# A fused decoder layer on one core: the order of the last eight slots, written out by hand on four engines

## The chip, the cores and the metric

The kernel runs on 1 core of one Trainium2 chip. The metric is the device time of one execution in microseconds; the time of a version is the median of its runs. A smaller time is better.

## The reference

x is 4 x 512 tokens of 512 channels, float32. The layer has three stages, each followed by a residual and a layernorm without weights:

```python
# 1: attention: four products with quantised rows and ternary weights, a linear recurrence over the tokens
x = _layernorm(x + _L0_attn_ref(x, Wi, Wf, Wg, Wo, g_norm_weight))
# 2: each token has one of 4 experts, by its token id
g = silu(h @ ctx[e].T); u = h @ ctx[e].T; y = (g * u) @ ctx[e]      # 512 x 512 for each expert
x = _layernorm(x + y)
# 3: mixed = sum over the 8 factors of x @ factor, / sqrt(8) + bias
x = _layernorm(x + mixed)
```

In stage 2 the gate, the up and the down weights are the same matrix of the expert, so that one product gives g and u: hidden = silu(z) * z.

## The kernel before

**Tiles, groups, slots.** The 2048 tokens are 16 tiles of 128, in 8 groups of two. The attention stage runs group by group, with channels on the partitions for the recurrence. Its normalised rows are scattered to DRAM (`sorted_rows`) in an order in which each block of 128 rows belongs to one expert. Such a block is a slot. There are N_SLOTS = 19, since four experts can leave three blocks partly filled. Stages 2 and 3 run slot by slot.

**One slot n**, step by step, with the engine of each:

- `load_rows(n)` (SP, L207 to L212): a DMA of 128 rows into `rows[n % 4]`. It waits for `square_2(n - 4)` and `token_of_row(n - 4)`, which were the last to read that buffer, and for the scatters that fill the slot.
- `transpose_a(n)` (PE, L1427): four 128 x 128 transposes of the rows into a PSUM bank. From slot 11 on (TAIL = 11) the bank is `bank_a`, and the step waits for `low_a(n - 1)`; before that it is `bank_tr`, which it shares with `transpose_h`.
- `high_a(n)` (ACT, L614) and `low_a(n)` (DVE, L985): the bank is split into a rounded part a_hi and the rest a_lo, both fp32r.
- `up(n)` (PE, L1467): z = a times the slot's expert, twelve matmuls of 512 columns into `bank_z`: eight that need a_hi, then four that need a_lo. It waits for `hidden(n - 1)`.
- `silu_z(n)` (ACT, L623) and `hidden(n)` (DVE, L994): act_z = silu(z) * z.
- `transpose_h(n)` (PE), `high_h(n)` (ACT), `low_h(n)` (DVE), `down(n)` (PE, into `bank_y`): the same pattern for the second product.
- `residual_2(n)` (DVE, L998): y plus the rows, with a sum along the row, and a small operation that makes the mean. `square_2(n)` (ACT, L628): the sum of squares. `power_2(n)` (POOL, L322, three small operations at L312 to L314): the scale. `norm_2(n)` (ACT, L634): the layernorm, in place in `x2[n % 4]`.
- `transpose_m(n)` (PE, into `bank_q`), `high_m(n)` (ACT), `low_m(n)` (DVE), `mix(n)` (PE, into `bank_m`, waits for `residual_3(n - 1)`): the third product, with the sum of the factors.
- `add_bias(n)` (POOL, L350): adds the bias to x2, after `transpose_m(n)`. `token_of_row(n)` (POOL, L346): keeps the token numbers of the slot's rows.
- `residual_3(n)` (DVE, L1008), with its small mean, which waits for `mix(n)`, `add_bias(n)` and for the landing of `store(n - 2)`; `square_3(n)` (ACT, L641), `power_3(n)` (POOL), `norm_3(n)` (ACT, L647).
- `store(n)` (POOL, L355): an indirect DMA of the rows to the output.

**What sets the order.** Every engine has its own list of steps, written out in the code, and takes them strictly in that order; semaphores hold a step until what it reads is there. For the slots up to 10 the lists run beside the attention groups: a loop over `turn`, and then a hand-written piece for the last group. From slot 11 on each engine ran a loop over n, printed below in the function: on PE `up(n)`, `transpose_a(n + 1)`, `transpose_m(n - 2)`, `down(n - 1)`, `transpose_h(n)`, `mix(n - 2)`. In the last rounds of the loop only the steps remain whose slot exists: `up(18)`, `transpose_m(16)`, `down(17)`, `transpose_h(18)`, `mix(16)`; then `transpose_m(17)`, `down(18)`, `mix(17)`; then `transpose_m(18)`, `mix(18)`. On POOL a round of the loop was `power_3(n - 3)`, `add_bias(n - 2)`, `store(n - 3)`, `token_of_row(n + 1)`, `power_2(n - 1)`.

Of the kernel before, what the change touches and what calls it, by code (L numbers as in the profile page):

```python
# [74 lines left out]
def decoder_layer(nc, x, small_in, ctx_t, wf_t, wi_t, wg_t, wo_t, g_weight, factors, bias, out):  # L75
# [6 lines left out]
    with ExitStack() as whole:  # L82
# [105 lines left out]
        def is_slot_n(n):  # L188
            return 0 <= n < N_SLOTS

        with nc.Block() as block:
# [49 lines left out]
            def _(pool):  # L241
# [252 lines left out]
                add_bias(n - 1)  # L494
                token_of_row(n + 1)

                token_of_row(TAIL)
                for n in range(TAIL, N_SLOTS + 3):
                    if is_slot_n(n - 3):
                        power_3(n - 3)  # L500
                    if is_slot_n(n - 2):
                        add_bias(n - 2)
                    if is_slot_n(n - 3):
                        store(n - 3)
                    if is_slot_n(n + 1):
                        token_of_row(n + 1)
                    if is_slot_n(n - 1):
                        power_2(n - 1)
                pool.wait_ge(s.out0, 16 * ((N_SLOTS + 1) // 2))
                pool.wait_ge(s.out1, 16 * (N_SLOTS // 2))  # L510

# [1 line left out]
            def _(act):  # L513
# [335 lines left out]
                norm_2(n)  # L849
                norm_3(n - 2)  # L850

                silu_z(TAIL - 1)
                high_h(TAIL - 1)
                high_a(TAIL)
                for n in range(TAIL, N_SLOTS + 3):
                    if TAIL - 1 <= n - 2 and is_slot_n(n - 2):
                        norm_2(n - 2)
                    if is_slot_n(n - 3):
                        square_3(n - 3)
                    if is_slot_n(n):  # L860
# [12 lines left out]
            @block.vector  # L873
            def _(dve):
# [777 lines left out]
```

## Time and profile before

| what | value |
|---|---|
| median of 3 runs | 341.45 us (340.44 to 343.64) |
| profiled execution, its own time | 342.06 us |
| its span, first to last instruction | 340.3 us |
| mean granted TensorE clock over the span | 0.963 |
| PE busy | 278.1 us (82%), 1505 matmuls |
| DVE busy | 226.3 us (66%) |
| ACT busy | 229.6 us (67%) |
| POOL busy | 190.8 us (56%) |

Times in the trace count from the first instruction. "Busy" is the union of an engine's instructions. A start in the timeline is when an instruction began on its engine; consecutive matmuls overlap, so that their pace is read from the distance of the starts. What stands in brackets is how long the engine had been idle before the instruction and what released it. A clock of 1.00 is 2.4 GHz, one of 0.50 is 1.2 GHz.

### The profile page before, as it was taken

The page shows a single profiled execution, that of the slowest core. Times are in us where ns is not written, and L with a number is a line of the kernel's source. Part 1 is how long each engine was busy: PE and PEld are TensorE (multiplying, and loading weights), DVE is VectorE, ACT ScalarE, POOL GpSimd, SP SyncE. Part 2 cuts the span into 40 slices and gives each one's busy share as a digit, 9 for nine tenths or more (in the row PEclk, how much of TensorE's full clock was granted, in tenths as well). Part 3 has the DMA queues.
Part 4 walks back from the last instruction along what each step waited for, and adds up shares of the span by engine and source line. Part 5 has one row for each costly group of instructions (what it writes and reads, how often), then busy time and mean ns, then how long its engine had stood idle before and what let it go on. Part 6 is the DMA issues. An engine that isn't in the chain of part 4 may idle for free.

```text
span 340.3 us, 5734 instructions
## 1 busy us (share of the span) xinstructions
PE 278.1 (82%) x1505; PEld 211.9 (62%) x1518; DVE 226.3 (66%) x488; ACT 229.6 (67%) x456; POOL 190.8 (56%) x381
## 2 busy tenths in 40 slices
PE   1376646484879899999999998998999999999760
PEld 1253414252557678787778876676888888887540
DVE  2789999999987879968677696454543434543310
ACT  4687789889678769986887686476555644554530
POOL 2536765858637748865565856547444444454442
PEclk9999989879799999999999999999999999999975
DMA  7999981987593782013003002205111111000000
GB/s 233 387 388 387 225 196 62 185 153 143 130 227 79 115 179 65 1 62 126 0 33 141 17 15 111 62 7 186 56 40 56 62 66 62 33 26 29 4 6 0
DMA packets 17406, 37.02 MB, mean 109 GB/s; under 512 B 1503, under 2 KB 1631, under 8 KB 17376
## 3 DMA queue, kind: packets, MB, share of 16 engines
q0 software_dynamic: 6496, 15.74, 19.6%
q1 hardware_dynamic: 10880, 20.92, 19.2%
q8 instruction: 14, 0.23, 0.3%
q14 instruction: 16, 0.13, 0.1%
HBM read 26.68 MB, written 10.76 MB: 110 GB/s over the span
## 4 chain that ended last, share of the span: by engine, by line
PE 62%; ACT 9%; issue 5%; DVE 5%; DMA 2%; POOL 2%; ACTq 0%; POOLq 0%; DVEq 0%; SPq 0%
PE bank_y L1455 5%; PE bank_z L1455 5%; PE bank_y L1456 5%; PE bank_z L1456 5%; PE bank_z L1459 5%; PE bank_y L1459 5%; PE bank_m L1455 4%; PE bank_m L1456 4%; PE bank_m L1459 4%; PE bank_tr L1424 3%; PE bank_c L1357 2%; PE bank_q L1424 2%; PE bank_a L1357 1%; PE bank_b L1357 1%; DMA sorted_rows<-r,place 1%
## 5 line engine op out<-in xcount | busy, mean ns | idle before, releaser
L312 POOL TENSOR_SCALAR n_v<-n_dev 128x1 f32<-128x1 f32 (+1 forms) x46 | 8.8, 192 | 52.2 <-ACT x L644 26.7
L1455 PE MATMUL bank_y<-c_hi,h_hi 128*128 x76 | 31.8, 418 | 1.8 <-ACT h_hi L612 1.4
L996 DVE TENSOR_TENSOR act_z<-bank_z,act_z 128x512 f32<-128x512 f32 x19 | 13.1, 689 | 30.1 <-ACT act_z L626 30.1
L1455 PE MATMUL bank_m<-f_hi,m_hi 128*128 128x512 f32 x76 | 32.1, 423 | 0.8 <-ACT m_hi L612 0.8
L353 POOL TENSOR_TENSOR x<-x,bias_b 128x512 f32<-128x512 f32 x19 | 24.6, 1293 | 14.5 <-PE bank_q L1424 14.5
L1455 PE MATMUL bank_z<-c_hi,a_hi 128*128 x76 | 30.4, 400 | 2.8 <-ACT a_hi L612 1.5
L1456 PE MATMUL bank_m<-f_lo,m_hi 128*128 128x512 f32 x76 | 30.8, 405 | 0.0
L1456 PE MATMUL bank_y<-c_lo,h_hi 128*128 x76 | 30.1, 396 | 0.0
L1456 PE MATMUL bank_z<-c_lo,a_hi 128*128 x76 | 30.1, 395 | 0.0
L612 ACT ACTIVATE h_hi<-bank_tr 128x512 fp32r<-128x512 f32 x19 | 11.3, 596 | 26.7 <-PE bank_tr L1424 26.7
L313 POOL TENSOR_TENSOR n_d<-n_v,minus_half 128x1 f32<-128x1 f32 (+1 forms) x46 | 27.1, 588 | 3.8
L358 POOL DMA_INDIRECT out<-r,token_of x19 | 20.3, 1067 | 12.3 <-ACT r L651 7.6
L1013 DVE SCALAR_TENSOR_TENSOR r<-bank_m,x 128x512 f32<-128x512 f32 x19 | 13.1, 691 | 21.0 <-PE bank_m L1459 20.0
L1002 DVE SCALAR_TENSOR_TENSOR x<-bank_y,rows 128x512 f32<-128x512 f32 x19 | 13.1, 691 | 19.1 <-PE bank_y L1459 19.1
L638 ACT ACTIVATE x<-x,n_b,n_d 128x512 f32<-128x512 f32 x19 | 15.4, 810 | 12.2 <-POOL n_b L314 12.2
L1357 PE MATMUL bank_c<-xq_t,w_q 128*128 128x256 bf16 x128 | 18.3, 291 | 5.2 <-ACT mc_row L540 2.7
L343 POOL DMA_INDIRECT sorted_rows<-r,place x16 | 17.8, 1113 | 8.3 <-ACT r L594 5.7
L1459 PE MATMUL bank_m<-f_hi,m_lo 128*128 128x512 f32 x76 | 21.3, 403 | 0.0
L1459 PE MATMUL bank_y<-c_hi,h_lo 128*128 x76 | 20.6, 393 | 0.0
L1459 PE MATMUL bank_z<-c_hi,a_lo 128*128 x76 | 20.6, 393 | 0.0
L644 ACT ACTIVATE x<-r,n_mean 128x512 f32<-128x512 f32 x19 | 13.7, 720 | 9.6 <-DVE n_mean L1017 9.6
L626 ACT ACTIVATE act_z<-bank_z 128x512 f32<-128x512 f32 x19 | 11.2, 592 | 12.1 <-PE bank_z L1459 12.1
(205 smaller groups left out, 848.7 us busy)
## 6 DMA issues: line engine op xcount, KB each, us to landing
f_sum<-in_factors POOLq DMA_DIRECT2D x7, 1024.0 KB
rows<-sorted_rows SPq DMA_DIRECT2D x19, 256.5 KB, 2.9
xs<-in_x SPq DMA_DIRECT2D x8, 512.0 KB, 7.6
c_stage<-in_ctx_t SPq DMA_DIRECT2D x4, 1024.0 KB, 14.3
sorted_rows<-pad_row SPq DMA_DIRECT2D x1, 1539.0 KB, 18.3
w_stage<-in_wf_t SPq DMA_DIRECT2D x1, 1024.0 KB, 8.7
w_stage<-in_wi_t SPq DMA_DIRECT2D x1, 1024.0 KB, 10.8
w_stage<-in_wg_t SPq DMA_DIRECT2D x1, 1024.0 KB, 13.0
```

What stands on the lines that cost most here:

```text
L313: link(pool.tensor_tensor(d, v, minus_half[:, 0:v.shape[1]], ALU.pow), chain)
L343: pool.indirect_dma_start(sorted_rows, bass.IndirectOffsetOnAxis(place[:, u:u + 1], 0), r1[:, j, :], None).then_inc(s_scat[j], 16)
L353: pool.tensor_tensor(tile, tile, bias_b[:], ALU.add).then_inc(s.x2b, 1)
L358: pool.indirect_dma_start(out_rows, bass.IndirectOffsetOnAxis(token_of[:, n:n + 1], 0), r3[:, n % 2, :], None, bounds_check=B * S - 1, oob ...
L638: a.activation(r, r, ACT.Identity, bias=n2_b[:, n % 2:n % 2 + 1], scale=n2_d[:, n % 2:n % 2 + 1]).then_inc(s.x2, 1)
L644: a.activation(x2[:, n % RING, :], r3[:, n % 2, :], ACT.Square, bias=n3_mean[:, n % 2:n % 2 + 1], accum_out=n3_dev[:, n % 2:n % 2 + 1]).th ...
L996: v.tensor_tensor(act_z[:], bank_z[:], act_z[:], ALU.mult).then_inc(s.hid, 1)
L1357: last = t.matmul(bank[:, i * GW:(i + 1) * GW], w_q[:, m, d, ch:ch + P], xq_t[:, :, d, :], start=(d == 0), stop=(d == KC - 1))
L1424: last = t.transpose(bank[:, c * P:(c + 1) * P], src[:, c * P:(c + 1) * P], ident[:])
L1455: t.matmul(bank[:], hi[:, c, :], w_hi(c), start=(c == 0), stop=False)
L1456: t.matmul(bank[:], hi[:, c, :], w_lo(c), start=False, stop=False)
L1459: last = t.matmul(bank[:], lo[:, c, :], w_hi(c), start=False, stop=(c == KC - 1))
```

## The change

Each engine's loop over the last slots is replaced by a written list of the same steps. No step is added or dropped and no wait, buffer or tile is changed: each engine issues the same instructions with the same semaphore counts, in another order. On PE `transpose_a(11)` now comes ahead of `transpose_h(10)`, `transpose_m(9)` ahead of `up(11)`, the transposes of the next rows stand right behind `up`, and at the end `transpose_m(17)` and `mix(17)` stand behind `down(18)`. The diff, with the indentation taken off and several of the new lines put into one:

```diff
@@ -1601,22 +1735,61 @@
-mix(TAIL - 3)
-transpose_h(TAIL - 1)
-transpose_a(TAIL)
-for n in range(TAIL, N_SLOTS + 2):
-    if is_slot_n(n):
-        up(n)
-    if is_slot_n(n + 1):
-        transpose_a(n + 1)
-    if is_slot_n(n - 2):
-        transpose_m(n - 2)
-    if is_slot_n(n - 1):
-        down(n - 1)
-    if is_slot_n(n):
-        transpose_h(n)
-    if is_slot_n(n - 2):
-        mix(n - 2)
+ mix(8); transpose_a(11); transpose_h(10); transpose_m(9); up(11); transpose_a(12); down(10); mix(9)
+ transpose_a(13); transpose_h(11); up(12); down(11); transpose_m(10); transpose_h(12); up(13)
+ transpose_a(14); mix(10); transpose_m(11); down(12); transpose_h(13); up(14); transpose_a(15); mix(11)
+ down(13); transpose_h(14); transpose_m(12); up(15); transpose_a(16); mix(12); transpose_h(15); down(14)
+ transpose_m(13); up(16); transpose_a(17); mix(13); transpose_h(16); transpose_m(14); down(15); up(17)
+ transpose_a(18); mix(14); transpose_m(15); down(16); up(18); transpose_h(17); mix(15); transpose_m(16)
+ down(17); transpose_h(18); mix(16); down(18); transpose_m(17); mix(17); transpose_m(18); mix(18)
@@ -849,26 +887,82 @@
-silu_z(TAIL - 1)
-high_h(TAIL - 1)
-high_a(TAIL)
-for n in range(TAIL, N_SLOTS + 3):
-    if TAIL - 1 <= n - 2 and is_slot_n(n - 2):
-        norm_2(n - 2)
-    if is_slot_n(n - 3):
-        square_3(n - 3)
-    if is_slot_n(n):
-        silu_z(n)
-    if is_slot_n(n + 1):
-        high_a(n + 1)
-    if is_slot_n(n - 2):
-        high_m(n - 2)
-    if is_slot_n(n - 3):
-        norm_3(n - 3)
-    if is_slot_n(n):
-        high_h(n)
-    if is_slot_n(n - 1):
-        square_2(n - 1)
+ silu_z(10); high_a(11); high_h(10); square_3(8); high_a(12); high_m(9); silu_z(11); square_2(10)
+ norm_3(8); norm_2(10); high_h(11); silu_z(12); square_3(9); high_a(13); high_m(10); high_h(12)
+ square_2(11); norm_2(11); high_a(14); high_m(11); silu_z(13); square_3(10); norm_3(9); high_h(13)
+ silu_z(14); norm_3(10); square_2(12); high_a(15); norm_2(12); high_m(12); square_2(13); high_h(14)
+ square_3(11); high_a(16); silu_z(15); norm_2(13); norm_3(11); square_3(12); high_h(15); square_2(14)
+ high_m(13); silu_z(16); norm_2(14); high_a(17); high_m(14); norm_3(12); square_3(13); high_h(16)
+ square_2(15); silu_z(17); norm_2(15); high_m(15); high_a(18); norm_3(13); square_2(16); square_3(14)
+ silu_z(18); norm_2(16); high_h(17); norm_3(14); high_m(16); square_2(17); high_h(18); square_3(15)
+ norm_2(17); square_3(16); norm_3(15); high_m(17); square_2(18); norm_3(16); norm_2(18); high_m(18)
+ square_3(17); norm_3(17); square_3(18); norm_3(18)
@@ -1283,22 +1377,62 @@
-hidden(TAIL - 1)
-low_h(TAIL - 1)
-low_a(TAIL)
-for n in range(TAIL, N_SLOTS + 3):
-    if is_slot_n(n - 3):
-        residual_3(n - 3)
-    if is_slot_n(n):
-        hidden(n)
-    if is_slot_n(n + 1):
-        low_a(n + 1)
-    if is_slot_n(n - 2):
-        low_m(n - 2)
-    if is_slot_n(n - 1):
-        residual_2(n - 1)
-    if is_slot_n(n):
-        low_h(n)
+ hidden(10); low_h(10); low_a(11); residual_3(8); hidden(11); low_a(12); low_m(9); residual_2(10)
+ residual_3(9); low_h(11); hidden(12); residual_2(11); low_a(13); low_m(10); low_h(12); low_a(14)
+ hidden(13); residual_3(10); low_h(13); residual_2(12); low_m(11); residual_3(11); hidden(14)
+ residual_2(13); low_a(15); low_h(14); low_m(12); hidden(15); low_a(16); residual_3(12); residual_2(14)
+ low_m(13); low_h(15); hidden(16); residual_3(13); residual_2(15); low_a(17); low_h(16); low_m(14)
+ low_a(18); hidden(17); low_m(15); residual_2(16); residual_3(14); hidden(18); residual_3(15); low_h(17)
+ low_m(16); residual_2(17); low_h(18); residual_3(16); residual_2(18); low_m(17); residual_3(17); low_m(18)
+ residual_3(18)
@@ -494,18 +494,56 @@
-token_of_row(TAIL)
-for n in range(TAIL, N_SLOTS + 3):
-    if is_slot_n(n - 3):
-        power_3(n - 3)
-    if is_slot_n(n - 2):
-        add_bias(n - 2)
-    if is_slot_n(n - 3):
-        store(n - 3)
-    if is_slot_n(n + 1):
-        token_of_row(n + 1)
-    if is_slot_n(n - 1):
-        power_2(n - 1)
+ power_3(8); add_bias(9); power_2(10); token_of_row(11); token_of_row(12); store(8); add_bias(10)
+ token_of_row(13); power_2(11); power_3(9); add_bias(11); token_of_row(14); token_of_row(15); store(9)
+ power_3(10); store(10); power_2(12); power_2(13); power_3(11); add_bias(12); add_bias(13); store(11)
+ power_2(14); add_bias(14); power_3(12); power_2(15); store(12); power_3(13); store(13); add_bias(15)
+ power_2(16); power_3(14); token_of_row(16); store(14); add_bias(16); power_2(17); token_of_row(17)
+ power_3(15); power_3(16); store(15); power_2(18); add_bias(17); store(16); add_bias(18); power_3(17)
+ token_of_row(18); store(17); power_3(18); store(18)
```

The four parts are those of PE, ACT, DVE and POOL. SP's list of loads is unchanged.

## Rows read from the trace of the kernel before

**Rows 1.** Busy time of the engines by stage: stretch, sum, PE, PEld, DVE, ACT, POOL, clock, DMA.
```profile
237.60:311.60 74.00, 74.00 (x365) 60.91 (x366) 32.72 (x76) 39.01 (x75) 34.02 (x68) 1.00 0.14 49
...
311.60:329.50 17.90, 15.12 (x61) 11.07 (x59) 5.51 (x16) 7.97 (x15) 9.01 (x17) 0.90 0.05 18
```

**Rows 2.** Timeline of TensorE, slot 11: start, us, what [idle before, releaser].
```profile
236.16 0.66 PE L1424 MATMUL bank_a<-small,rows 128*128 128x128 f32 x4 [0.40 <-DMA rows<-sorted_rows]
...
237.60 0.49 PE L1455 MATMUL bank_z<-c_hi,a_hi 128*128 x1 [0.78 <-ACT a_hi L612]
...
240.48 0.60 PE L1424 MATMUL bank_a<-small,rows 128*128 128x128 f32 x4
...
241.27 0.48 PE L1455 MATMUL bank_y<-c_hi,h_hi 128*128 x1
...
244.50 0.48 PE L1455 MATMUL bank_m<-f_hi,m_hi 128*128 128x512 f32 x1
...
247.38 0.39 PE L1455 MATMUL bank_z<-c_hi,a_hi 128*128 x1
...
250.17 0.60 PE L1424 MATMUL bank_a<-small,rows 128*128 128x128 f32 x4
```

**Rows 3.** Timeline of TensorE at the end.
```profile
313.87 1.10 PE L1459 MATMUL bank_m<-f_hi,m_lo 128*128 128x512 f32 x4
...
315.67 0.66 PE L1424 MATMUL bank_q<-small,x 128*128 128x128 f32 x4 [0.70 <-ACT x L638]
...
316.43 0.49 PE L1455 MATMUL bank_y<-c_hi,h_hi 128*128 x1
...
319.31 0.39 PE L1455 MATMUL bank_m<-f_hi,m_hi 128*128 128x512 f32 x1
...
323.43 0.66 PE L1424 MATMUL bank_q<-small,x 128*128 128x128 f32 x4 [1.14 <-ACT x L638]
...
324.86 0.47 PE L1455 MATMUL bank_m<-f_hi,m_hi 128*128 128x512 f32 x1 [0.78 <-ACT m_hi L612]
```

**Rows 4.** Timeline of DVE, ACT and POOL at the end.
```profile
319.51 0.69 DVE L1002 SCALAR_TENSOR_TENSOR x<-bank_y,rows 128x512 f32<-128x512 f32 x1 [1.56 <-PE bank_y L1459]
...
320.44 0.72 ACT L631 ACTIVATE rows<-x,n_mean 128x512 f32<-128x512 f32 x1 [1.58 <-DVE n_mean L1006]
...
322.56 0.81 ACT L638 ACTIVATE x<-x,n_b,n_d 128x512 f32<-128x512 f32 x1 [1.31 <-POOL n_b L314]
...
324.12 0.60 ACT L612 ACTIVATE m_hi<-bank_q 128x512 fp32r<-128x512 f32 x1
...
329.48 0.69 DVE L1013 SCALAR_TENSOR_TENSOR r<-bank_m,x 128x512 f32<-128x512 f32 x1 [4.04 <-PE bank_m L1459]
...
331.38 0.19 POOL L312 TENSOR_SCALAR n_v<-n_dev 128x1 f32<-128x1 f32 x1 [3.33 <-ACT x L644]
```

**Rows 5.** Busy time by stretch; PE's granted clock stands third from the end.
```profile
325.50:325.75 0.25, 0.25 (x3) 0.15 (x2) 0.00 (x0) 0.25 (x1) 0.25 (x1) 0.50 0.00 0
```

**Rows 6.** Timeline of ACT and DVE, slot 17.
```profile
298.84 0.60 ACT L626 ACTIVATE act_z<-bank_z 128x512 f32<-128x512 f32 x1 [1.06 <-PE bank_z L1459]
...
299.47 0.69 DVE L996 TENSOR_TENSOR act_z<-bank_z,act_z 128x512 f32<-128x512 f32 x1 [2.54 <-ACT act_z L626]
...
300.08 0.68 DVE L983 TENSOR_TENSOR a_lo<-bank_a,a_hi 128x512 fp32r<-128x512 f32 x1
```

**Rows 7.** Timeline: the small mean on DVE, beside POOL's add_bias and alone.
```profile
221.99 1.28 POOL L353 TENSOR_TENSOR x<-x,bias_b 128x512 f32<-128x512 f32 x1 [1.61 <-PE bank_q L1424]
222.02 1.27 DVE L972 TENSOR_SCALAR n_mean<-n_sum 128x2 f32<-128x2 f32 x1
...
320.25 0.15 DVE L1006 TENSOR_SCALAR n_mean<-n_sum 128x1 f32<-128x1 f32 x1
```

**Rows 8.** Line 358 (store): its issue on POOL, and from issue to landing.
```profile
326.99 1.07 POOL L358 DMA_INDIRECT out<-r,token_of  x1 [0.41 <-issue]
...
DMA to landing us min/median/max: 2.2/2.8/5.3
```

More of the change, by code:

```diff
@@ L495, in _ @@
                 token_of_row(n + 1)
-                token_of_row(TAIL)
-                for n in range(TAIL, N_SLOTS + 3):
-                    if is_slot_n(n - 3):
-                        power_3(n - 3)
-                    if is_slot_n(n - 2):
-                        add_bias(n - 2)
-                    if is_slot_n(n - 3):
-                        store(n - 3)
-                    if is_slot_n(n + 1):
-                        token_of_row(n + 1)
-                    if is_slot_n(n - 1):
-                        power_2(n - 1)
+                power_3(8)
+                add_bias(9)
+                power_2(10)
+                token_of_row(11)
+                token_of_row(12)
+                store(8)
+                add_bias(10)
+                token_of_row(13)
+                power_2(11)
+                power_3(9)
+                add_bias(11)
+                token_of_row(14)
+                token_of_row(15)
+                store(9)
+                power_3(10)
+                store(10)
+                power_2(12)
+                power_2(13)
+                power_3(11)
+                add_bias(12)
+                add_bias(13)
+                store(11)
+                power_2(14)
+                add_bias(14)
+                power_3(12)
+                power_2(15)
+                store(12)
+                power_3(13)
+                store(13)
+                add_bias(15)
+                power_2(16)
+                power_3(14)
+                token_of_row(16)
+                store(14)
+                add_bias(16)
+                power_2(17)
+                token_of_row(17)
+                power_3(15)
+                power_3(16)
+                store(15)
+                power_2(18)
+                add_bias(17)
+                store(16)
+                add_bias(18)
+                power_3(17)
+                token_of_row(18)
+                store(17)
+                power_3(18)
+                store(18)
                 pool.wait_ge(s.out0, 16 * ((N_SLOTS + 1) // 2))
@@ L850, in _ @@
                 norm_3(n - 2)
[L852 to L871 removed]
+                silu_z(10)
@@ new lines, in _ @@
+                high_a(11)
+                high_h(10)
+                square_3(8)
+                high_a(12)
+                high_m(9)
+                silu_z(11)
+                square_2(10)
+                norm_3(8)
+                norm_2(10)
+                high_h(11)
+                silu_z(12)
+                square_3(9)
+                high_a(13)
+                high_m(10)
+                high_h(12)
+                square_2(11)
+                norm_2(11)
+                high_a(14)
@@ new lines, in _ @@
+                high_m(11)
+                silu_z(13)
+                square_3(10)
+                norm_3(9)
+                high_h(13)
+                silu_z(14)
+                norm_3(10)
+                square_2(12)
+                high_a(15)
+                norm_2(12)
+                high_m(12)
+                square_2(13)
+                high_h(14)
+                square_3(11)
+                high_a(16)
+                silu_z(15)
+                norm_2(13)
+                norm_3(11)
@@ new lines, in _ @@
+                square_3(12)
+                high_h(15)
+                square_2(14)
+                high_m(13)
+                silu_z(16)
+                norm_2(14)
+                high_a(17)
+                high_m(14)
+                norm_3(12)
+                square_3(13)
+                high_h(16)
+                square_2(15)
+                silu_z(17)
+                norm_2(15)
+                high_m(15)
+                high_a(18)
+                norm_3(13)
+                square_2(16)
@@ new lines, in _ @@
+                square_3(14)
+                silu_z(18)
+                norm_2(16)
+                high_h(17)
+                norm_3(14)
+                high_m(16)
+                square_2(17)
+                high_h(18)
+                square_3(15)
+                norm_2(17)
+                square_3(16)
+                norm_3(15)
+                high_m(17)
+                square_2(18)
+                norm_3(16)
+                norm_2(18)
+                high_m(18)
+                square_3(17)
@@ L873, in _ @@
+                norm_3(17)
+                square_3(18)
+                norm_3(18)
             @block.vector
```

110 lines of the change are left out of this document (added).

## The prediction

> **What bounds the kernel now.** The numbers are read in four steps. First the busy time by stage: from 237.60 to 311.60, while the slots from 11 on run, PE is busy 74.00 of 74.00 us at the full granted clock, and DVE, ACT and POOL are busy less than 40 us each [rows 1]. So what bounds the last eight slots is TensorE's own work, and no order of the same instructions can shorten it; it can only take away idle PE at the two ends. From 311.60 to 329.50 PE is idle 2.8 of 17.9 us [rows 1].
>
> Second, one slot of PE [rows 2]. A product (12 matmuls of 512 columns) takes 2.88 behind a transpose (237.60 to 240.48, and 244.50 to 247.38) and 2.79 behind another product (247.38 to 250.17). Two groups of four transposes ahead of a product take 0.79 (240.48 to 241.27); with the 0.09 by which the product behind them is longer that is 0.44 a group, 0.35 of it before the product starts. Three products and three groups make 9.69 a slot (240.48 to 250.17); I use 2.79 and 0.44 throughout. The reader is to see also that the first transpose of slot 11 starts at 236.16 because its rows landed only then, and that up(11) follows 1.44 later, after ACT has made a_hi (0.78 of that is put down to ACT).
>
> Third, the drain on PE [rows 3]. mix(16) would hand over at 313.87 + 0.92 = 314.79, but the transpose of m(17) starts at 315.67: 0.88 idle, 0.70 of it put down to ACT's norm. down(18) starts 0.76 after that, where 0.35 is usual: 0.40 more. mix(17) runs from 319.31, then PE waits until 323.43 for m(18) and until 324.86 for m_hi.
>
> Fourth, who makes it wait [rows 4]. From down(18)'s end at 319.31: residual at 319.51 (+0.20), square at 320.44 (+0.93), norm at 322.56 (+2.12, POOL's three small steps in it), transpose at 323.43 (+0.87), m_hi at 324.12 (+0.69), mix(18) at 324.86 (+0.74): 5.55 together. Then mix(18) itself is slow. From its start at 324.86 to residual_3 at 329.48 it takes 4.62, where down(18) took 316.43 to 319.51, or 3.08, for the same twelve matmuls [rows 3, 4]. The reason stands in the windows: from 325.50 the granted clock is 0.50 [rows 5], so most of mix(18) ran at 1.2 instead of 2.4 GHz. Before the fall PE had been without work from 322.10 (319.31 + 2.79) to 323.43 and again from the end of the transposes to 324.86. The low clock costs 1.54.
>
> **The change part by part.** No instruction is added or taken away; the counts of products, transposes, DMAs and elementwise operations are the same, so all that counts is where each queue waits.
>
> Start. transpose_h(10) and transpose_m(9) now stand behind transpose_a(11), which sits until 236.16. They run at 236.60 and 237.04 in the 1.44 that PE waits for a_hi anyway [rows 2]. h(10) had been in the wait for the rows; m(9) had cost 0.44 inside the slot. Gain 0.44. x(9) is long ready, since norm_2(9) is issued before the tail. On DVE low_h(10) still stands ahead of low_a(11): h_hi is made only at about 237.9, so a_lo(11) is done at about 239.2, and up(11) asks for it after 8 matmuls of 0.233, at 239.46. Margin 0.2.
>
> Middle. I walked PE through the new list without gaps: up(11) 237.60, down(10) 240.84, mix(9) 243.71, up(12) 247.30, up(13) 253.76, up(14) 263.45, up(15) 273.14, up(16) 282.83, up(17) 292.60, up(18) 301.85, down(17) 308.23, mix(16) 311.46, down(18) 314.33, its end 317.12 (all that follows counts from this walk; the 0.25 found below shifts all together). For each transpose I then followed its operand through ACT, DVE and POOL in their new orders, with 0.60 from one DVE operation to the next, 0.63 from silu_z to hidden [rows 6], 0.49 for a copy on ACT (estimate: the 0.60 of a copy overlaps the next start by about 0.1, as on DVE), 0.72 for a square or norm, and 2.12 from square to norm [rows 4]. Most operands have over half a microsecond to spare. The tight ones: transpose_m(12), because store(10) now stands ahead of power_2(12) on POOL (norm_2(12) at 271.8, transpose possible at 272.7, nominal 272.78); a_lo(17), because low_a(17) waits behind residual_2(15) (done 294.4, asked 294.46); up(18), which asks for hidden(17), and that stands behind low_a(18), high_a(18) and high_m(15) (done 301.7, nominal 301.85); h_hi(18) behind square_2(17) (margin 0.6). None of these is over its time.
>
> One thing is. The small mean behind a residual takes 0.15 alone (320.25), but one of its kind takes 1.27 where it starts inside POOL's add_bias: 222.02 against 221.99 + 1.28 [rows 7]. Before, the tail has no such meeting. In the walk the new order has three: the mean of slot 11 (at 253.9, in add_bias(10), 253.6 to 254.9), of slot 14 (283.4, in add_bias(13), 283.2 to 284.4) and the third mean of slot 14 (303.9, in add_bias(15)). Each holds DVE for 0.4 to 1.05. At slots 14 nothing behind it is due. At slot 11 low_a(13) comes at 255.1 instead of 254.1 and is done at 255.8, where up(13) asks for it at 253.76 + 1.86 = 255.62: PE loses 0.25 with the hand-off. I cost the middle at 0.25. Lower bound 0 (the meeting is missed by some tenths); upper bound four slips of 0.5, or 2.0, since what PE loses there it never gets back.
> The Trainium skill (SBUF — State Buffer, Who interferes with whom) says that VectorE in its two-port modes, which a tensor_scalar can enter, and GpSimd take a shared pair of ports by turns, each for a whole instruction, and that an operation with one input in SBUF outside these modes does not meet GpSimd. The trace agrees: the mean waits until add_bias is over, the residual and hidden, whose other input is a PSUM bank, never do. By this rule the three meetings are real and the time is the sum below; without it, it would be 0.25 lower.
>
> SP's queue: rows(n) asks for square_2(n-4) and token_of_row(n-4). These stay at least 7 us ahead of transpose_a(n) in the walk; a cost of 0. Of the stores, residual_3(n) asks that store(n-2) has landed: 2.8 us in the median, at most 5.3 [rows 8]. store(15) starts at about 318.0 in the walk, lands at 320.8, and is asked at 321.6; at 5.3 it would cost 1.7.
>
> Up to down(18)'s end. Before, 319.31. Less the idle 0.88 and 0.40, less m(9)'s 0.44, less m(17)'s 0.44, which now comes behind down(18): 317.15 (the walk gives 317.12). Gain 2.19. This is a gain only if the middle holds.
>
> Behind down(18). Now: transpose_m(17) at once, 1.43 to mix(17) as from 323.43 to 324.86, mix(17) 2.87, transpose_m(18), 1.43 to mix(18): 5.73, against 5.55 before. x(18) takes 4.1 from down(18)'s end, and high_m(17) on ACT (copy from 317.8) stands just ahead of square_2(18) (wanted 318.25): no loss, 0.1 to spare. store(15) ahead of power_2(18) ends at 319.1 and the power is wanted at 319.3. So mix(17) no longer covers all of the last chain, and the last chain covers mix(17): loss 0.18, mix(18) at 322.85.
>
> The clock. In the new order PE's idle stretches here are 317.8 to 318.55, and after mix(17) about 322.1 to 322.85, with matmuls of 2.87 between. Before the fall at 325.50 there was 1.3 and 0.8 of idle with only four transposes between [rows 3, 5]. I take it that the clock stays full: mix(18) takes 3.08 to residual_3 instead of 4.62, gain 1.54. Bounds: 0 (falls as early in mix(18) as before) and 1.54.
>
> Last queue. POOL's list ends add_bias(17), store(16), add_bias(18), power_3(17), store(17), power_3(18), store(18). With 1.28 for add_bias [rows 7], 0.41 + 1.07 for a store [rows 8], 1.15 for a power (2.12 less the 0.97 from square to POOL: 1.90 from residual_3 to power_3 less 0.93 [rows 4]), power_3(17) ends at 325.7, norm_3(17) at 326.5, store(17) runs until 328.4. residual_3(18) is at 325.93, so power_3(18) is wanted at 327.83 and gets POOL at 328.4: loss 0.6. Before, store(17) was away at 326.99 + 1.07, long before 331.38 [rows 4, 8]. From power_3(18) to the end nothing changes.
>
> Sum: -2.19 + 0.25 + 0.18 - 1.54 + 0.6 = -2.70. The profiled execution took 342.06 with a span of 340.3, so the new one is 339.4 with a span of 337.6. The median of the runs is 341.45, 0.6 below the profiled one; part of that may be that the clock falls later or not at all in other runs. I keep 339.4 as the time, 2.05 or 0.6% under the median.
>
> **The rivals.**
> A. More than 1% faster: POOL is free for power_3(18) in time (my 0.6 is too much), no mean meets an add_bias, and the timed runs of before all lose the clock as the profiled one: 341.45 - 2.70 - 0.6 - 0.25 = 337.9. For it: POOL is busy only 34.02 of 74.00 [rows 1]. Against: five POOL operations stand in a row, each near its time.
> B. The clock falls in mix(18) all the same: 339.4 + 1.5 = 340.9. For it: two waits of 0.75 stay. Against: a whole mix between them.
> C. The middle leaks. Three queues now have margins of 0.1 to 0.6 at the places named above. With the upper bound of the middle, 2.0 in place of 0.25, the time is 341.1, and the change shows nothing. For it: the hand-offs are added up from single rows, each good to some 0.05. Against: a slip moves all queues together, so that several do not add up fully.
> D. Slower. POOL is held by its stores. The new list puts store(10) ahead of power_2(12), store(11) ahead of power_2(14), store(13) of power_2(16), store(15) of power_2(18) and store(17) of power_3(18), where a store stood behind the power before. If a store held POOL until it lands, 2.8 instead of 1.07 [rows 8], that is 1.7 more at each place: at m(12) and m(18) with margin 0.1 all but 0.1 counts (1.6 each), at m(14) and m(16) with margins of about 1.4 some 0.3 each, at power_3(18) the whole 1.7: 5.5, so 344.9, over 1% above the median. It turns slower than before once a store holds POOL for about 0.8 more than 1.07. Against: the stores show 1.07 on POOL and a median landing of 2.8 side by side [rows 8], so the engine goes on.
>
> **How the numbers follow.** The forecast has 0.50 (own range 338.4 to 340.4: store and clock terms either way), A 0.15, B 0.12, C 0.16, D 0.07. Range 337.7 to 342.3: it takes in B, C and most of A, and leaves out most of D and the end of A. A measurement of this kernel can tell about 1%, or 3.4 us, from no change. Faster by more than that: A and a little of the forecast, 0.17. Slower by more: half of D and a worse case of C, 0.05. Within: 0.78.
>
> **What would show it.** Right: a PE busy nearly all of 237.6 to about 317, down(18) ending near 317.4; one mean on DVE of over 1 us beside an add_bias; one wait of about 0.8 ahead of mix(17), none ahead of the transpose of m(18); the granted clock at 1.00 through mix(18), and residual_3(18) 3.1 after its start; a late power_3(18) whose releaser is not ACT's square but POOL's own store. Wrong: PE idle ahead of transpose_m(12), up(17) or up(18) by more than 0.3; a clock of 0.50 behind 322; a residual_3 that waits for the DMA of a store; or PE work in the middle longer than 9.69 a slot.

## The result, and the profile after

The changed kernel takes 340.17 us (median of 13 runs, 338.74 to 341.30) where the kernel before takes 341.59 beside it (13 runs, 339.59 to 343.64): a ratio of 0.9960, interval 0.9943 to 0.9978. That is 0.4% faster, against 0.6% forecast. The interval leaves out no change, but the step is less than the 1% that the prediction took a measurement of this kernel to tell. The profiled execution took 340.39 us.

The page of the changed kernel, its span and the busy time of each engine:
```profile
span 338.6 us, 5747 instructions
...
PE 281.4 (83%) x1518; PEld 213.2 (63%) x1518; DVE 225.5 (67%) x488; ACT 229.3 (68%) x456; POOL 192.3 (57%) x381
```
The busy times are those of before within 3.3 us (the counts of PE differ by records that a trace drops). The span is 1.7 shorter. The two executions do not start the tail together, though: the first transpose of slot 11 stands at 236.66, and stood at 236.16 [rows 2]. Its rows come from a scatter far ahead of the change. So everything below is counted from that transpose. From it to the end of the span it was 340.3 - 236.16 = 104.14 before, and is 338.6 - 236.66 = 101.94 now: 2.20 gained, where 2.70 was forecast.

Busy time by stretch, changed kernel (columns as in [rows 1]; the first stretch is the start of slot 11, the second ends where up(18) starts):
```profile
236.66:238.10 1.44, 1.44 (x13) 1.30 (x13) 0.00 (x0) 0.75 (x2) 1.44 (x3) 1.00 0.90 318
238.10:303.18 65.08, 64.64 (x317) 52.60 (x317) 28.68 (x66) 33.00 (x64) 25.67 (x55) 1.00 0.14 48
303.18:317.20 14.02, 14.02 (x66) 11.43 (x67) 6.54 (x19) 7.80 (x16) 8.19 (x18) 1.00 0.09 36
317.20:324.26 7.06, 5.50 (x28) 4.11 (x26) 2.52 (x8) 4.79 (x10) 5.17 (x9) 1.00 0.09 36
```
PE now works through the start, and through all of the stretch ahead of the last waits. In the long second stretch, where before it was busy for 74.00 of 74.00 us [rows 1], it is idle for 0.44. This is where. TensorE of the changed kernel at up(18), then at the end (start, us, what):
```profile
301.65 1.09 PE L1593 MATMUL bank_y<-c_hi,h_lo 128*128 x4
303.18 0.49 PE L1589 MATMUL bank_z<-c_hi,a_hi 128*128 x1 [0.44 <-issue]
...
317.68 1.09 PE L1593 MATMUL bank_y<-c_hi,h_lo 128*128 x4
318.61 0.60 PE L1558 MATMUL bank_q<-small,x 128*128 128x128 f32 x4
319.99 0.47 PE L1589 MATMUL bank_m<-f_hi,m_hi 128*128 128x512 f32 x1 [0.78 <-ACT m_hi L650]
...
322.88 0.60 PE L1558 MATMUL bank_q<-small,x 128*128 128x128 f32 x4
324.26 0.48 PE L1589 MATMUL bank_m<-f_hi,m_hi 128*128 128x512 f32 x1 [0.78 <-ACT m_hi L650]
```
down(16) hands over at 301.65 + 0.93 = 302.58 (0.93 is the usual distance from the last four matmuls of a product to the next one), and up(18) starts at 303.18, 0.60 later. The 0.44 in the row is the same gap, counted from where the trace draws the end of the last matmul; below it is taken as 0.60. At the end the waits of 0.88 ahead of the transpose of m(17) and of 1.14 ahead of that of m(18) [rows 3] are gone. What stays is 0.78 ahead of each mix. down(18) ends at 318.61, which is 81.95 behind the transpose of slot 11, against 83.15 before.

What up(18) waits for, ACT and DVE of the changed kernel:
```profile
299.99 0.60 ACT L650 ACTIVATE m_hi<-bank_q 128x512 fp32r<-128x512 f32 x1 [1.91 <-PE bank_q L1558]
300.48 0.59 ACT L650 ACTIVATE a_hi<-bank_a 128x512 fp32r<-128x512 f32 x1
...
301.11 0.69 DVE L1077 TENSOR_TENSOR a_lo<-bank_a,a_hi 128x512 fp32r<-128x512 f32 x1 [4.51 <-ACT a_hi L650]
301.72 0.68 DVE L1090 TENSOR_TENSOR act_z<-bank_z,act_z 128x512 f32<-128x512 f32 x1
```
ACT's high_m(15) stands ahead of high_a(18), DVE's low_a(18) ahead of hidden(17). DVE has idled for 4.51 before low_a(18), and hidden(17) is over at 302.40. up(18) then needs another 0.78.

The last mix, busy time by stretch from its start to residual_3(18), first of before, then of after:
```profile
324.86:329.48 4.62, 4.58 (x12) 3.29 (x12) 0.58 (x1) 0.81 (x1) 2.71 (x4) 0.63 0.04 12
```
```profile
324.26:327.34 3.08, 3.04 (x12) 2.15 (x12) 0.58 (x2) 1.11 (x3) 2.48 (x6) 1.00 0.02 2
```
The same twelve matmuls, at a mean clock of 0.63 and at 1.00: 1.54 apart. Behind them, POOL of the changed kernel:
```profile
328.55 1.09 POOL L358 DMA_INDIRECT out<-r,token_of  x1 [1.53 <-ACT r L689]
329.71 0.19 POOL L312 TENSOR_SCALAR n_v<-n_dev 128x1 f32<-128x1 f32 x1
...
332.48 1.07 POOL L358 DMA_INDIRECT out<-r,token_of  x1 [1.65 <-ACT r L689]
```
power_3(18) starts right behind store(17), 2.37 after residual_3(18) (329.71 - 327.34), where it was 1.90 [rows 4].

### The profile page after: what moved, and what is told of

It reads as the page before. It is cut to its first block, busy times and chain, and to the rows that moved or that the text cites. A ratio compares the mean times of both kernels' runs of the same rounds, so it can differ in the third digit from the quotient of the medians.

```text
span 338.6 us, 5747 instructions
## 1 busy us (share of the span) xinstructions
PE 281.4 (83%) x1518; PEld 213.2 (63%) x1518; DVE 225.5 (67%) x488; ACT 229.3 (68%) x456; POOL 192.3 (57%) x381
## 4 chain that ended last, share of the span: by engine, by line
PE 62%; ACT 7%; issue 5%; DVE 5%; POOL 3%; DMA 2%; POOLq 0%; ACTq 0%; DVEq 0%; SPq 0%
PE bank_z L1589 5%; PE bank_y L1589 5%; PE bank_z L1590 5%; PE bank_z L1593 5%; PE bank_y L1590 5%; PE bank_y L1593 5%; PE bank_m L1589 4%; PE bank_m L1593 4%; PE bank_m L1590 4%; PE bank_tr L1558 4%; PE bank_c L1491 3%; PE bank_q L1558 2%; PE bank_a L1491 1%; PE bank_m L1553 1%; PE bank_a L1558 1%
## 5 line engine op out<-in xcount | busy, mean ns | idle before, releaser
L1590 PE MATMUL bank_m<-f_lo,m_hi 128*128 128x512 f32 x76 | 30.1, 396 | 0.0
L1491 PE MATMUL bank_c<-xq_t,w_q 128*128 128x256 bf16 x128 | 19.3, 302 | 4.8 <-POOL w_q L298 2.6
L669 ACT ACTIVATE rows<-x,n_mean 128x512 f32<-128x512 f32 x19 | 13.7, 721 | 12.5 <-DVE n_mean L1100 12.5
L1077 DVE TENSOR_TENSOR h_lo<-bank_tr,h_hi 128x512 fp32r<-128x512 f32 x19 | 13.1, 687 | 11.7 <-ACT h_hi L650 11.7
L650 ACT ACTIVATE m_hi<-bank_q 128x512 fp32r<-128x512 f32 x19 | 11.3, 593 | 13.3 <-PE bank_q L1558 10.9
L689 ACT ACTIVATE r<-r,n_b,n_d 128x512 f32<-128x512 f32 x19 | 15.3, 807 | 6.9 <-POOL n_b L314 6.9
```

Of the source, the lines that this page charges most:

```text
L669: a.activation(rows[:, n % RING, 0:D], x2[:, n % RING, :], ACT.Square, bias=n2_mean[:, n % 2:n % 2 + 1], accum_out=n2_dev[:, n % 2:n % 2 + ...
L689: a.activation(r, r, ACT.Identity, bias=n3_b[:, n % 2:n % 2 + 1], scale=n3_d[:, n % 2:n % 2 + 1]).then_inc(s.x3, 1)
L1077: v.tensor_tensor(flat(lo[:]), bank[:], flat(hi[:]).bitcast(F32), ALU.subtract).then_inc(s_done, 1)
L1491: last = t.matmul(bank[:, i * GW:(i + 1) * GW], w_q[:, m, d, ch:ch + P], xq_t[:, :, d, :], start=(d == 0), stop=(d == KC - 1))
L1590: t.matmul(bank[:], hi[:, c, :], w_lo(c), start=False, stop=False)
```

## The experiments

For each kernel one execution was profiled. In this table "to down(18)" and "to the end" count from the first transpose of slot 11, in us; the ratio is to the kernel before on the same chip, in timed runs. A median is to be held against the kernel before on its own chip, whose median lay between 341.55 and 342.55, and not against the other rows. The ratio is the one on record, over the runs beside each other, and not the quotient of two medians (for kernel 5 that would be 0.9961).

| kernel | median (runs) | ratio, interval | to down(18)'s end | to the end |
|---|---|---|---|---|
| before | 341.59 (13) | 1 | 83.15 | 104.14 |
| before, profiled again | 341.03 (1) | | 83.16 | 102.58 |
| after | 340.17 (13) | 0.9960 (0.9943 to 0.9978) | 81.95 | 101.94 |
| after, timed again | 340.90 (12) | 0.9959 (0.9930 to 0.9988) | 81.97 | 101.97 |
| 1: offset loaded early | 340.79 (8) | 0.9962 (0.9930 to 0.9995) | 81.49 | 101.54 |
| 2: high_a(18) first | 338.44 (2) | 0.9893 (0.9835 to 0.9951) | 81.23 | 101.23 |
| 2, timed again | 338.77 (6) | 0.9912 (0.9884 to 0.9940) | 81.18 | 101.14 |
| 3: store(17) late | 340.28 (8) | 0.9952 (0.9921 to 0.9984) | 81.91 | 101.70 |
| 4: only the end reordered | 340.64 (12) | 0.9949 (0.9922 to 0.9975) | 81.47 | 101.31 |
| 5: waits filled in before | 341.23 (12) | 0.9946 (0.9924 to 0.9969) | 83.16 | 102.57 |
| two columns behind the mean | 340.94 (1) | | 82.05 | 102.09 |
| 6: both ends | 339.91 (6) | 0.9922 (0.9897 to 0.9946) | 81.02 | 100.67 |
| 6, timed again | 340.12 (12) | 0.9924 (0.9899 to 0.9949) | 81.21 | 100.85 |
| 7: all repairs in after | 343.11 (12) | 1.0043 (1.0011 to 1.0074) | 81.48 | 101.19 |

**1 and 2. What up(18) waits for.** Theory: the wait for hidden(17), and the load of the slot's weight offset into a register, which stands behind that wait. Kernel 1 puts the load first, in up and down:
```diff
-def expert_product(n, bank, hi, lo, s_hi, s_lo, s_done):
+def expert_product(n, bank, hi, lo, s_hi, s_lo, s_done, free):
     at = pe.value_load(slot_off[0:1, n:n + 1], ...)
+    after(pe, free, n)
...
 def up(n):
-    after(pe, s.hid, n)
```


> The kernel after, with the load of the slot's offset into a PE register placed ahead of the wait on hidden (up) and on residual_2 (down), where it stood behind it. Theory (the load's latency is exposed where PE has to wait): in the profile of after, up(18) starts 0.77 us behind the end of hidden(17), while a mix starts 0.14 behind the end of its copy; so up(18) should start 0.15 to 0.25 behind hidden(17), PE idle ahead of it 0.1 instead of 0.60, and the span should be about 0.5 shorter measured from transpose_a(11). Rival (the hand-off from DVE to PE itself takes this long): up(18) starts 0.7 to 0.8 behind hidden(17) as before, nothing changes.

Kernel 2 leaves the wait and makes hidden(17) early, by one swap on ACT:
```diff
-high_m(15)
 high_a(18)
+high_m(15)
```


> The kernel after, with high_a(18) ahead of high_m(15) on ACT. Theory (up(18) waits because hidden(17) stands behind low_a(18), that behind high_a(18), and that behind high_m(15), which needs a transpose made 3.3 us after that of a(18)): hidden(17) ends some 2 to 3 us earlier, up(18) follows down(16) with no idle PE, 0.6 less from transpose_a(11) to the end of down(18). Rival (up(18) waits for its own register load or for something on PE): the 0.6 stays.

Measured in kernel 1, with DVE's hidden(17) and PE's next weight load and matmul:
```profile
302.41 0.68 DVE L1090 TENSOR_TENSOR act_z<-bank_z,act_z 128x512 f32<-128x512 f32 x1
...
303.23 0.19 PEld L1589 LDWEIGHTS bank_z<-c_hi,a_hi 128*128 128x128 f32 x1 [0.23 <-issue]
303.27 0.47 PE L1589 MATMUL bank_z<-c_hi,a_hi 128*128 x1
```
From the end of hidden(17), 303.09, to the matmul it is 0.18 now, 0.78 in the changed kernel (0.82 in its second profile): so the load in between costs at least 0.60. (It may cost more: down(16) hands over at 302.35 + 0.93 = 303.28 here, so the 0.18 is PE's own work and no wait at all.) hidden(17) itself had not been late in the changed kernel: 302.40, when PE was free at 302.58. In kernel 2, DVE's hidden(17), then TensorE:
```profile
298.32 0.68 DVE L1090 TENSOR_TENSOR act_z<-bank_z,act_z 128x512 f32<-128x512 f32 x1
...
300.76 1.09 PE L1593 MATMUL bank_y<-c_hi,h_lo 128*128 x4
301.69 0.39 PE L1589 MATMUL bank_z<-c_hi,a_hi 128*128 x1
```
hidden(17) is over at 299.00, 2.5 earlier than in the changed kernel when both are counted from slot 11's transpose, and up(18) follows down(16) after 0.93, without a wait. down(18) ends 0.46 sooner in kernel 1, and 0.72 and 0.77 sooner in the two profiles of kernel 2. So the loss is there, and either half of its cause, the load behind the wait or the late hidden(17), can be taken away. In kernel 1 up(11) and up(15) each start 0.10 later behind the transposes ahead of them than in the changed kernel. That the early load does this is not shown: the second profile of kernel 6, with the load where it was, has up(11) 0.19 later. In timed runs kernel 1 cannot be told from the changed kernel (0.9962 against 0.9960).

**3. store(17) behind power_3(18).** On POOL, in the changed kernel:
```diff
-store(17)
 power_3(18)
+store(17)
```


> The kernel after, with store(17) behind power_3(18) on POOL. Theory (power_3(18) is held by the store ahead of it): from residual_3(18) to power_3(18) 1.90 us as in the kernel before, instead of 2.37; the last store is issued about 0.4 to 0.5 earlier. Rival (the two stores then stand back to back, and the second is held by the first's issue): power_3(18) earlier by 0.47, but the last store no earlier than 5.1 us behind residual_3(18), as in after.

Measured, on POOL:
```profile
328.83 0.19 POOL L312 TENSOR_SCALAR n_v<-n_dev 128x1 f32<-128x1 f32 x1 [2.22 <-ACT x L682]
...
330.52 1.09 POOL L358 DMA_INDIRECT out<-r,token_of  x1 [0.61 <-issue]
331.92 0.98 POOL L358 DMA_INDIRECT out<-r,token_of  x1 [0.30 <-issue]
```
power_3(18) is on time, 1.90 behind residual_3(18) at 326.93. But now store(17) holds store(18): the last one starts 4.99 behind residual_3(18), 5.14 in the changed kernel, 4.66 before. So store(17) is in the way on either side of power_3(18). It has to be gone before, which asks for an earlier norm_3(17).

**4. Only the end.** The kernel before, its loops stopped after round 18, and the rest written out. On PE (the other three lists are written out to match):
```diff
-for n in range(TAIL, N_SLOTS + 2):
+for n in range(TAIL, N_SLOTS):
...
+down(18); transpose_m(17); mix(17); transpose_m(18); mix(18)
```


> The kernel before, with its loops kept up to round 18 and only the end written out: down(18) ahead of transpose_m(17) and mix(17) on PE, residual_2(18) ahead of low_m(17) on DVE, square_2(18) ahead of norm_3(16) on ACT, power_2(18) ahead of add_bias(17) and store(16) on POOL. Theory (the whole gain lies in the end, and the new order of the middle only adds a leak of 1.0): end of down(18) 81.4 us behind the start of transpose_a(11) (before 83.15, after 81.95), no idle PE ahead of it, the granted clock 1.00 through mix(18), and 101.3 from transpose_a(11) to the end of the span (before 104.14, after 101.94); median about 339.7, 0.5% under before. Rival (the transposes moved ahead of products in the middle carry a part of the gain): 0.5 or more slower than after from transpose_a(11).

Measured: 81.47 and 101.31, against 81.4 and 101.3 expected. This kernel keeps the loops in the middle, and of the start's gain it has nothing, yet its down(18) ends 0.48 sooner than the changed kernel's. Its time cannot be told from that of the changed kernel. So the transposes that were moved in the middle carry nothing of the gain.

**5. The clock by itself.** The kernel before, with matmuls that nothing reads put into PE's two waits ahead of mix(18):
```diff
+    if n == N_SLOTS + 1:
+        filler(5)
     transpose_m(n - 2)
...
+    if n == N_SLOTS + 1:
+        filler(3)
     mix(n - 2)
```


> The kernel before, with 8 matmuls added that no one reads (5 behind mix(17), 3 behind the transposes of m(18), 0.233 us each, into bank_z), inside the two waits of 1.33 and 0.77 us ahead of mix(18). Theory (the low clock in mix(18) comes from PE being without work there, and is a part of what the change gains): granted clock 1.00 through mix(18), 3.08 from its start to residual_3(18) instead of 4.62, and 102.6 from transpose_a(11) to the end instead of 104.14; the median under before by what the clock costs there on average, 0.8 if it falls in half of the executions, 1.5 if in all. Rival (the fall is a matter of where in time the program stands, and not of the waits): the clock falls as before, no difference.

The kernel before, as it is, was profiled again beside it:

> The kernel before, unchanged, looked at once more. Theory (the fall in mix(18) depends on how the waits lie against the chip's own timing, which differs between executions, so the profile of before shows one case of several): from mix(18)'s start to residual_3(18) anything from 3.08 to 4.62, with the fall of the clock at another distance from mix(18)'s start than the 0.64 of the first profile. Rival (it is the same in each execution): 4.62 again.

TensorE of kernel 5:
```profile
322.50 1.10 PE L1459 MATMUL bank_m<-f_hi,m_lo 128*128 128x512 f32 x4
323.44 1.33 PE L1486 MATMUL bank_z<-f_hi,a_hi 128*128 128x512 f32 x5
324.74 0.66 PE L1424 MATMUL bank_q<-small,x 128*128 128x128 f32 x4
325.15 0.94 PE L1486 MATMUL bank_z<-f_hi,a_hi 128*128 128x512 f32 x3
```
Then mix(18) keeps the full clock, and from slot 11 to the end it is 102.57, as expected:
```profile
326.17:329.25 3.08, 3.04 (x12) 2.15 (x12) 0.58 (x2) 0.82 (x1) 2.59 (x4) 1.00 0.00 0
```
But the second profile of the kernel before, without any filler, shows this:
```profile
325.25:328.34 3.09, 3.05 (x12) 2.15 (x12) 0.58 (x2) 0.82 (x1) 2.60 (x4) 1.00 0.00 0
```
The clock is 1.00 over the whole of mix(18) there too, behind the same waits (1.13 and 0.78). So the kernel before loses 1.54 in some executions and not in others; in two profiles it was once each way. The twelve profiles of kernels whose end is reordered or filled all have residual_3(18) within 3.07 to 3.31 of mix(18)'s start. So this profile of kernel 5 proves nothing of the filler by itself. In timed runs kernel 5 is faster than before (ratio 0.9946, medians 1.32 apart), clear of noise, and the 1.32 is within the 0.8 to 1.5 expected. The filler adds only work to PE, so this speaks for a clock that falls in many runs of the kernel before; but another build also starts slot 11 at another time (237.43 here, 236.16 and 236.52 before), and the runs do not tell the two apart.

**The small mean.** The changed kernel, with one more small operation behind the mean, of two columns instead of one, in the slots from 11:
```diff
 the mean of residual_2(n), 128 x 1
+if n >= TAIL:
+    v.tensor_scalar(x_mr[:], minus_half[:], -1.0 / D, None, ALU.mult)   # 128 x 2
```


> The kernel after, with one more small operation on DVE behind the mean of slots 11 to 18: the same tensor_scalar, on 128x2 float32 in SBUF instead of 128x1, its output read by no one. Theory (what waited for add_bias in the rows of before was the 128x2 form; the 128x1 form does not take the ports): where it falls into an add_bias, as in slot 11 (add_bias(10) 17.5 to 18.8 us behind transpose_a(11), the mean at 17.7), the 128x2 operation takes until the end of add_bias, 0.9 to 1.0, and the 128x1 mean just ahead of it 0.15. Rival (small operations do not wait here at all, the 1.27 of before had another cause): both take 0.15.

Measured at slot 11, where POOL's add_bias(10) runs from 254.63 to 255.91:
```profile
254.63 1.28 POOL L353 TENSOR_TENSOR x<-x,bias_b 128x512 f32<-128x512 f32 x1 [4.44 <-PE bank_q L1560]
```
```profile
254.87 0.15 DVE L1100 TENSOR_SCALAR n_mean<-n_sum 128x1 f32<-128x1 f32 x1
254.94 1.00 DVE L1102 TENSOR_SCALAR x_mr<-minus_half 128x2 f32<-128x2 f32 x1
255.85 0.68 DVE L1077 TENSOR_TENSOR a_lo<-bank_a,a_hi 128x512 fp32r<-128x512 f32 x1
```
Side by side, inside the same add_bias: one column takes 0.15, two columns take 1.00, until add_bias is over. The two columns met an add_bias at three slots (1.00, 1.00 and 1.31) and took 0.16 to 0.20 elsewhere. In the changed kernel itself three means of one column start inside an add_bias (at 254.40, 284.09 and 304.48), as the prediction's walk had it; each takes 0.15 or 0.16.

**6. Both ends, loops between.** Kernel 4, with the start as in the change (PE: transpose_a(11), transpose_h(10), transpose_m(9), then the loop; ACT: high_a(11) ahead of high_h(10)), and with power_3(17) ahead of add_bias(18) on POOL:
```diff
-transpose_h(TAIL - 1)
 transpose_a(TAIL)
+transpose_h(TAIL - 1)
+transpose_m(TAIL - 2)
...
-add_bias(18)
 power_3(17)
+add_bias(18)
```


> The end-only kernel, with the start as in the change (transpose_a(11), transpose_h(10), transpose_m(9) ahead of up(11), and high_a(11) ahead of high_h(10)), and power_3(17) ahead of add_bias(18) on POOL. Theory (the gain is in the two ends, the order of the middle is not needed): 0.44 less on PE for transpose_m(9), about 0.2 less ahead of power_3(18): 100.7 from transpose_a(11) to the end, against 101.31 for the end alone and 101.94 for after; median about 339.3 to 339.8. Rival (the middle's loop, started 0.44 earlier, runs into the waits that the hand order avoids): 101.1 or more.

and in a second build, on another chip and beside the changed kernel:

> The simple version once more, beside the mended hand order and after, for the time on the same chip: 100.67 from transpose_a(11) to the end as before; median 0.7 to 1.3 under that of after. Rival (its first median was a lucky one): within 0.3 of after.

> The kernel after once more, for comparison on the same chip: 101.9 from transpose_a(11) to the end, the clock 1.00 through mix(18) again (PE's two waits there are 0.8 each with a whole product between), up(18) 0.77 behind hidden(17) again. Rival for the clock: now and then it falls here too, 103.5.

Measured: 101.94 becomes 100.67 and 100.85. Against kernel 4, down(18) ends 0.45 and 0.26 sooner, where 0.44 was expected of the start; in the second profile up(11) began 0.19 late. Behind that, the only waits of PE are the two of 0.78 ahead of the last mixes. POOL at the end of kernel 6:
```profile
327.05 1.07 POOL L358 DMA_INDIRECT out<-r,token_of  x1 [0.41 <-issue]
328.63 0.19 POOL L312 TENSOR_SCALAR n_v<-n_dev 128x1 f32<-128x1 f32 x1 [0.51 <-ACT x L653]
```
store(17) is over at 328.12, and power_3(18) comes 1.90 behind residual_3(18) (326.73). The price is 0.15: add_bias(18), now late, holds residual_3(18) until 3.24 after mix(18)'s start. On the second chip the medians are 340.12 for kernel 6 and 340.90 for the changed kernel, 0.8 apart, of the size that the profiles say (101.97 - 100.85 = 1.12); the two intervals (0.9899 to 0.9949 and 0.9930 to 0.9988) overlap, so the timed difference is not clear of noise.

**7. All repairs in the hand-written order**: the changed kernel with the edits of 1 and 2 and the POOL edit of 6.

> The kernel after with its three faults mended: the offset's load ahead of the wait, high_a(18) ahead of high_m(15), power_3(17) ahead of add_bias(18). Theory (the hand order of the middle has nothing to give beyond a gapless PE, which the loop has already): 80.9 to 81.0 from transpose_a(11) to the end of down(18) and 100.6 from there to the end of the span, equal to the simple version (81.02 and 100.67) within 0.15, so no difference of the two that can be measured. Rival (with the faults out the hand order is the better one): 100.3 or less.

It came out slower than before, at 1.0043. In its profile the part from slot 11 on is not slow: 101.19, which is better than the changed kernel (though 0.6 over the 100.6 expected; 0.3 of it at up(15), and 0.23 at residual_3(18), which add_bias(18) delays). What stands ahead of slot 11, the last scatter, the load of the rows (SPq is SyncE's queue) and the transpose:
```profile
230.51 0.96 POOL L343 DMA_INDIRECT sorted_rows<-r,place  x1 [0.30 <-issue]
235.48 1.33 SPq L212 DMA_DIRECT2D rows<-sorted_rows  x3
238.71 0.55 PE L1558 MATMUL bank_a<-small,rows 128*128 128x128 f32 x3 [2.26 <-DMA rows<-sorted_rows]
```
The rows of slot 11 are 2.05 later than in the changed kernel's first profile, after a wait of 2.26. From the scatter to the load it is 4.97 here, 4.07 in kernel 1 and 4.19 in the changed kernel profiled beside it. Up to there this kernel issues the same steps as kernel 1, and kernel 1 has the rows at 237.16 and is not slower than before.

But this does not account for the median. The profiled execution of kernel 7 took 341.72, the fastest of its twelve, and that of the changed kernel beside it took 342.18, with slot 11 at 238.43; the medians are 343.11 and 340.90. So no kept profile shows a slow execution of kernel 7. Where its median loses 2.2, and why, stays open.

Kernel 2, of which there were two timed runs, over six:

> The kernel after with high_a(18) ahead of high_m(15), timed in full. Theory (the swap is worth its 0.6 of PE and the rest of its two first times, 338.44, was where transpose_a(11) happened to start in them, 235.8): 101.2 from transpose_a(11) to the end as in its first profile, median 0.4 to 0.8 under after's ratio, so ratio to before 0.992 to 0.994, like the simple version. Rival (this build really starts slot 11 earlier, as the build of the mended hand order starts it later): ratio 0.989 again.

Measured 0.9912 (0.9884 to 0.9940): between the two expectations, and the interval holds both. In the profile it ends 101.14 behind the transpose of slot 11, as the theory says. The profiles give the swap 0.7 to 0.8, or 0.2%; the ratio is 0.5% under that of the changed kernel (0.9960 and 0.9959). Slot 11 starts at 235.77 and 236.26 in its two profiles, at 236.66 and 238.43 in those of the changed kernel, so a part of the timed gain may lie ahead of slot 11.

## Why the prediction was right, and where it was not

The side, the size of under 1% and the mechanisms at both ends were right; the sum was -2.70 and the profile shows -2.20. The median alone bears out little: the range of 337.7 to 342.3 held the time of no change as well, and the measured 1.42 hangs on how often the kernel before loses the clock in timed runs, for which the prediction had no more than a guess of 0.6. That the median came out near is in part luck. Point by point:

- **PE bounds, so only idle PE at the ends can be won (-2.19): right.** Kernel 6, whose middle has no gap, ends down(18) 81.02 behind the first transpose of slot 11 (81.21 in its second profile, with 0.19 lost at up(11)); the walk had 80.96.
- **The middle (+0.25): mis-sized, and for the wrong reason.** Up to down(18)'s end the profile shows 83.15 - 81.95 = 1.20 gained, so the middle cost 0.99. Nothing of that is the meeting of the small mean with add_bias(10). The mean did start inside it (254.40, in 254.16 to 255.45) and took 0.16, as did the two others. The failed step is "one of its kind takes 1.27": the row in [rows 7] has two columns, the mean behind residual_2 has one, and the last experiment on it shows that only the form with two columns waits. The Trainium skill (VectorE: DVE Perf Modes, What auto-detection actually checks) makes the two-port mode depend on the outermost dimension other than one being even, or equal for source and destination; two columns have such a dimension, one column has none. The trace agrees in that 128 x 2 waits, and shows that 128 x 1 does not.
- **Where the middle did lose.** I had named up(18) as tight (done 301.7, nominal 301.85) and let it pass: a margin of 0.15, with nothing between hidden(17) and the matmul. hidden(17) was over at 302.40, nominal 301.85 + 0.67 = 302.52 by then, so the operand was indeed in time, and the hand-off was 0.78. This is the second step that failed: the hand-off behind a wait, a term that the walk did not have. That is 0.60 idle, and 0.10 more by which the first matmul after a wait is longer (0.33 to the next instead of 0.23). The 0.67 is the 0.50 of the later start and 0.17 lost at up(15), behind a transpose of m(12) that I had put at "possible 272.7, nominal 272.78" (what up(15) waited for was not tested). The rest, 0.12, is put down to the walk's roundings. So 0.60 + 0.10 + 0.17 + 0.12 = 0.99. The other tight places, a_lo(17) and h_hi(18), cost nothing. This is rival C at half its upper bound.
- **Behind down(18) (+0.18): 5.65 instead of 5.55, +0.10.** No wait stands ahead of the transpose of m(18), as said.
- **The clock (-1.54): right in the profile, not in the median.** mix(18) took 3.08 instead of 4.62. But the second profile of before has it at 3.09, so the timed runs of before may hold only a part of that loss, of which the prediction had warned in one sentence and then taken 0.6 for it. From slot 11 to the end before has 104.14 or 102.58, after 101.94: a gain of 2.20 or 0.64 by execution. The measured 1.42 between the medians lies between them. How often the clock falls was not counted, and the record does not say whether the two profiles of before are of one chip.
- **The last queue (+0.6): 2.37 instead of 1.90, +0.47**, and POOL's own store is what it came behind, as said.
- **Stores do not hold POOL until they land (rival D): right.** From slot 11 on each held it for 1.07 to 1.09, with the landing at 2.8 in the median. The landing of store(15) held nothing: residual_3(17) waited for add_bias(17), which is what released it at 323.23, and PE did not notice.

Together: -2.19 + 0.99 + 0.10 - 1.54 + 0.47 = -2.17, the 2.20 of the profile but for rounding. Where the expected gain went: 0.7 of it into the one wait at up(18), which the order of ACT and DVE created. How much more of it went into the reference, which does not lose the clock each time, is not shown.

The hand-written order of the middle brings nothing: a part of PE that is full already cannot be made fuller, it can only leak. The loops with a written start and end (kernel 6) beat the changed kernel in the profile by 1.1 to 1.3 and in the timed medians by 0.8, which is not clear of noise; the changed kernel with the single swap on ACT is as good in timed runs (0.9912 against 0.9922 and 0.9924), and 0.3 to 0.6 behind kernel 6 in the profiles.

## What to carry to other kernels

Where one engine is busy all of a stretch, look for the gain at the ends of the stretch, and leave the order inside alone: what was moved there in this kernel only added a wait. In a walk through a new order, an operand that is "just in time" is late as soon as something must run between the wait and the first instruction that uses it; look for register loads behind a wait, and try them ahead of it. And profile the reference twice before counting on a loss in it that the clock makes.

## What the runs showed of the hardware

- **A register load behind a wait cost TensorE 0.6 at up(18).** With it behind the wait it was 0.78 from the end of hidden(17) to the next matmul, with it ahead 0.18. In kernel 2, with the load still behind the wait but hidden(17) over 2.7 before up(18), it cost nothing: 0.93 from the last four matmuls of down(16) to up(18).
- **A tensor_scalar of one column on DVE runs beside GpSimd's add_bias (0.15), one of two columns waits it out (1.00 to 1.31).**
- **The clock is not the same from one execution to the next of one kernel**, with the same waits ahead (1.14 and 0.78, 1.13 and 0.78): 0.63 and 1.00 in the mean over the same product. Whether the execution or the chip makes the difference is not shown.
- **Two stores in a row on POOL**: 1.40 from start to start (330.52 to 331.92).
- **The start of slot 11 moves by up to 2.9 between kernels whose steps up to it are nearly the same** (235.77 to 238.71), and by 1.77 between two profiles of the changed kernel itself (236.66 and 238.43). This is more than the whole change is worth, and what makes it was not found (the last scatter ahead of it itself starts at 229.32 in kernel 2 and at 231.49 in the changed kernel's second profile, and from there to the load it is 3.73 and 4.19); a comparison of two spans has to take it out first.
